# Second half of layer 0: LayerNorm's powers for four tiles at once, gathers ahead of stores, and rows kept for eight tiles

## The reference

```python
edge_index = jnp.stack([src, dst])
h = jnp.maximum(_layernorm(x, axis=-1), 0.0)
x = x + _L0_gnn_ref(h, edge_index, L0_gnn_W1, L0_gnn_b1, L0_gnn_W2, L0_gnn_b2)
...
def gnn_layer(x, W, b, src, dst):
    h = x @ W.T + b
    msgs = h[src]
    agg = jax.ops.segment_sum(msgs, dst, num_segments=N_NODES)
    return jax.nn.relu(agg)
h = gnn_layer(x, W1, b1, src, dst)
out = gnn_layer(h, W2, b2, src, dst)
```

## Time and profile before

| | |
|---|---|
| median of 3 runs | 2921.37 us (2920.29 to 2921.51) |
| the profiled execution | 2921.05 us, span 2919.0 us |
| granted TensorE clock, mean | 0.982 |
| busy: TensorE, VectorE, ScalarE, GpSimd | 89%, 70%, 46%, 60% of the span |
| second half of layer 0, first to last `add_x` | 769.0 to 1136.0 us |

### The profile page before, as it was taken

How to read it: one execution, slowest core, us unless ns; L and a number is a source line. 1 busy time by engine, 2 the same in 40 slices (tenths; PEclk the granted TensorE clock), 3 DMA queues, 4 the chain that set the end, 5 groups by cost and what they waited for, 6 DMA issues and landing times. The chain is left out here.

```text
span 2919.0 us, 51172 instructions
## 1 busy us (share of the span) xinstructions
PE 2596.8 (89%) x13954; PEld 2165.5 (74%) x13954; DVE 2056.6 (70%) x5472; ACT 1354.5 (46%) x2798; POOL 1754.9 (60%) x1917
## 2 busy tenths in 40 slices
PE   3677729999799996999999979999999889999998
PEld 2344427888677775889999967888888768888886
DVE  7688846666466564677778877888888746666666
ACT  0555414444455554655555534333333245555554
POOL 0455525555477776677777747877777555555554
PEclk9999999999899998999999999999999989999999
DMA  9544453333344444333333314443333255555553
GB/s 291 195 147 161 147 167 92 104 115 121 107 130 141 152 154 154 102 113 116 109 117 116 118 61 137 125 122 112 110 116 115 73 143 153 153 152 154 151 154 114
DMA packets 146573, 387.71 MB, mean 133 GB/s; under 512 B 34423, under 2 KB 35383, under 8 KB 145882
## 3 DMA queue, kind: packets, MB, share of 16 engines
q0 software_dynamic: 101408, 304.38, 35.0%
q1 hardware_dynamic: 44010, 80.12, 8.3%
q10 hardware_dynamic: 1056, 2.10, 0.2%
HBM read 261.74 MB, written 149.28 MB: 141 GB/s over the span
## 5 line engine op out<-in xcount | busy, mean ns | idle before, releaser
L1517 PE MATMUL c_pu<-c_Zhi,parts 128*128 128x256 f32 x640 | 182.3, 285 | 10.2 <-DVE c_Zlo L1442 10.2
L1519 PE MATMUL c_pu<-c_Zhi,parts 128*128 128x256 f32 x640 | 181.6, 284 | 0.0
L787 POOL DMA_INDIRECT f_Gsrc<-rows,indexS x80 | 80.6, 1007 | 166.3 <-PE f_phsrc L2013 160.4
L1518 PE MATMUL c_pu<-c_Zlo,parts 128*128 128x256 f32 x640 | 180.5, 282 | 0.0
L1955 DVE TENSOR_TENSOR f_Hlosrc<-f_phsrc,f_Hhisrc 128x512 fp32r<-128x512 f32 x80 | 55.4, 692 | 167.9 <-ACT f_Hhisrc L1925 137.2
L1931 ACT ACTIVATE f_Mhi<-f_pm 128x512 fp32r<-128x512 f32 x80 | 47.9, 599 | 267.2 <-DVE f_pm L1964 253.8
L791 POOL DMA_INDIRECT h<-a_rows,indexD x80 | 80.5, 1007 | 125.2 <-ACT a_rows L1103 116.9
L1679 ACT CAST d_Hhi<-d_ph 128x512 fp32r<-128x512 f32 x80 | 46.8, 585 | 227.7 <-PE d_ph L1793 222.9
L767 PE MATMUL a_po<-parts,a_Thi 128*128 128x512 f32 x320 | 132.6, 414 | 5.5 <-DVE a_Tlo L1135 5.4
L1409 ACT ACTIVATE c_pu<-c_pu,c_b1col 128x256 f32<-128x256 f32 x160 | 61.8, 450 | 162.9 <-PE c_pu L1519 162.9
L426 POOL DMA_INDIRECT edgesD<-r_cargoD,r_posiD x80 | 76.9, 961 | 97.0 <-ACT r_cargoS L473 40.4
(11 more groups left out here) (434 smaller groups left out, 9801.9 us busy)
## 6 DMA issues: line engine op xcount, KB each, us to landing
rows<-r_xt SPq DMA_DIRECT2D x20, 1040.0 KB
h<-q_zerorow SPq DMA_DIRECT2D x80, 256.0 KB, 2.3
r_xt<-in_x SPq DMA_DIRECT2D x80, 256.0 KB
selrowsD<-selD SPq DMA_DIRECT2D x1, 2640.0 KB
selrowsS<-selS SPq DMA_DIRECT2D x1, 2640.0 KB
q_keyrowD<-in_dst POOLq DMA_DIRECT2D x1, 2560.0 KB
q_keyrowS<-in_src POOLq DMA_DIRECT2D x1, 2560.0 KB
o_wstage<-in_L_W ACTq DMA_DIRECT2D x2, 1024.0 KB
```

The costliest lines, as they stand in the source:

```text
L787: return pool.indirect_dma_start(out, None, table, bass.IndirectOffsetOnAxis(ap=rows, axis=0))
L1517: pe.matmul(psum_u[:, o, :], g.Whi[2][:, c, cols], Zhi[:, c, :], start=c == 0, stop=False)
L1518: pe.matmul(psum_u[:, o, :], g.Whi[2][:, c, cols], Zlo[:, c, :], start=False, stop=False)
L1519: ins = pe.matmul(psum_u[:, o, :], g.Wlo[2][:, c, cols], Zhi[:, c, :], start=False, stop=c == C - 1)
```

## The change

In the second half of layer 0 the class `Norm` now takes a group of four tiles in place of two: VectorE's two small operations and GpSimd's power and multiply cover 128x4. `b_rows` has eight slots instead of four, and with it GpSimd's and VectorE's code is unrolled over eight tiles. A tile's order on GpSimd was store of T-2, G of T+4, xr of T+2, with power and multiply for T-2 and T-1 ahead of each pair. It is now G of T+4, xr of T+2, store of T-4, with power and multiply for T-4 to T-1 ahead of each four. The constant zeros behind the rows are written by one fill in place of four. `layer1` and `layer2` keep groups of two, and the first half of layer 0 keeps its order.

```diff
 class Norm:
-    def __init__(self, e, name, moved):
-        self.moved = moved
+    def __init__(self, e, name, moved, group=2):
+        self.moved, self.group, self.places = moved, group, 2 * group
...
     def finish(self, dve, tick, T):
-        s = T.slot(4)
-        wait(dve, self.s_bias if self.moved else self.s_scale, T.use(2) - 1)
+        s = T.slot(self.places)
+        some = slice(s - self.group + 1, s + 1)
+        wait(dve, self.s_bias if self.moved else self.s_scale, T.use(self.group) - 1)
...
-        if T.j % 2:
+        if T.j % self.group == self.group - 1:
             dve.wait_ge(self.s_mean, T.t + 1)
-            dve.tensor_scalar(self.var[:, s - 1:s + 1], self.mean_var[:, s - 1:s + 1, 1], LN_EPS, None, ALU.add)\
+            dve.tensor_scalar(self.var[:, some], self.mean_var[:, some, 1], LN_EPS, None, ALU.add)\
...
     def make_scales(self, pool, T, neg_half, scales):
-        s = T.slot(4)
-        pool.wait_ge(self.s_var, T.t // 2 + 1)
-        pool.tensor_tensor(scales, self.var[:, s:s + 2], neg_half[:, :], ALU.pow).then_inc(self.s_scale, 1)
+        s = T.slot(self.places)
+        pool.wait_ge(self.s_var, T.t // self.group + 1)
+        pool.tensor_tensor(scales, self.var[:, s:s + self.group], neg_half[:, :], ALU.pow).then_inc(self.s_scale, 1)
...
+    QUAD, RING = 4, 8 if second else 4
...
-        rows = e.sb("rows", [P, U, EXT if second else D], F32)
+        rows = e.sb("rows", [P, RING, EXT if second else D], F32)
...
             def body(i):
-                for pair in (0, 2):
-                    if second:
-                        at(i, pair, -2, U, NT, scales)
-                    for u in (pair, pair + 1):
+                if second:
+                    for u in range(RING):
+                        if u % QUAD == 0:
+                            at(i, u, -QUAD, RING, NT, scales)
+                        at(i, u, 4, RING, NT, start_fetch)
+                        at(i, u, 2, RING, NT, residual)
+                        at(i, u, -QUAD, RING, NT, store)
+                else:
+                    for u in range(U):
                         at(i, u, -2, U, NT, store)
                         at(i, u, 4, U, NT, start_fetch)
-                        if second:
-                            at(i, u, 2, U, NT, residual)
...
             def add_x(T):
-                s, r = T.slot(2), T.slot(U)
+                s, x, r = T.slot(2), T.slot(U), T.slot(RING)
                 dve.wait_ge(s_prod, T.t + 1)
-                dve.wait_ge(s_x[T.slot(U)], 16 * (T.use(U) + 1))
-
-                wait(dve, s_put[r], 16 * T.use(U))
+                dve.wait_ge(s_x[x], 16 * (T.use(U) + 1))
+
+                wait(dve, s_put[r], 16 * T.use(RING))
...
-            pipeline(dve, GR, 1, 1, body)
+            pipeline(dve, NT // RING, 1, 1, body)
```

More of the change, by code:

```diff
@@ L795 @@
 class Norm:
-    def __init__(self, e, name, moved):
-        self.moved = moved
+    def __init__(self, e, name, moved, group=2):
+        self.moved, self.group, self.places = moved, group, 2 * group
         self.stats = e.ring(name + "stats", 2, [P, 6], F32)
-        self.mean_var = e.sb(name + "mv", [P, 4, 2], F32)
-        self.var = e.sb(name + "var", [P, 4], F32)
-        self.minus = e.sb(name + "minus", [P, 4], F32) if moved else None
+        self.mean_var = e.sb(name + "mv", [P, self.places, 2], F32)
+        self.var = e.sb(name + "var", [P, self.places], F32)
+        self.minus = e.sb(name + "minus", [P, self.places], F32) if moved else None
         self.s_stats, self.s_mean, self.s_var, self.s_minus, self.s_scale, self.s_bias = (
@@ L807, in mean @@
     def mean(self, T):
-        return self.mean_var[:, T.slot(4), 0:1]
+        return self.mean_var[:, T.slot(self.places), 0:1]
     def statistics(self, dve, T, rows):
@@ L932, in layer0 @@
             brow = e.sb("brow", [P, D], F32)
[L933 removed]
+        neg_half = e.sb("neghalf", [P, QUAD], F32)
         G = e.ring("G", U, [P, D if second else EXT], F32)
@@ L937, in layer0 @@
         Thi, Tlo = e.ring("Thi", 2, [P, C, P], F32R), e.ring("Tlo", 2, [P, C, P], F32R)
-        rows = e.sb("rows", [P, U, EXT if second else D], F32)
+        rows = e.sb("rows", [P, RING, EXT if second else D], F32)
         xr = e.ring("xr", U, [P, D], F32) if second else None
-        ln = Norm(e, "ln", True) if second else None
+        ln = Norm(e, "ln", True, QUAD) if second else None
         W = None if second else Weights(nc, e, g, [(2, io.L1_W1), (3, io.L1_W2)])
@@ L1008, in scales @@
             def scales(T):
-                s = T.slot(U)
-                ln.make_scales(pool, T, neg_half, rows[:, s:s + 2, SCALE])
-                ln.make_biases(pool, T, rows[:, s:s + 2, SCALE], rows[:, s:s + 2, BIAS])
+                some = slice(T.slot(RING), T.slot(RING) + QUAD)
+                ln.make_scales(pool, T, neg_half, rows[:, some, SCALE])
+                ln.make_biases(pool, T, rows[:, some, SCALE], rows[:, some, BIAS])
             def store(T):
-                s = T.slot(U)
+                s = T.slot(RING)
                 if second:
-                    pool.wait_ge(ln.s_bias, T.t // 2 + 1)
+                    pool.wait_ge(ln.s_bias, T.t // QUAD + 1)
                 else:
@@ L1040, in _ @@
             if second:
-                for s in range(U):
-                    pool.memset(rows[:, s, BIAS + 1:EXT], 0.0).then_inc(s_const, 1)
-            pool.wait_ge(s_const, 3 + U if second else 3)
-            straight(GR, 1, 1, body, between=W and (lambda n: W.split_low(pool, n)))
-            for s in range(U):
-                pool.wait_ge(s_put[s], 16 * GR)
+                pool.memset(rows[:, :, BIAS + 1:EXT], 0.0).then_inc(s_const, 1)
+            pool.wait_ge(s_const, 4 if second else 3)
+            straight(NT // RING, 1, 1, body, between=W and (lambda n: W.split_low(pool, n)))
+            for s in range(RING):
+                pool.wait_ge(s_put[s], 16 * (NT // RING))
         @block.scalar
@@ L1155, in norm_rows @@
                 dve.wait_ge(s_rows, T.t + 1)
-                ln.statistics(dve, T, rows[:, T.slot(U), 0:D])
+                ln.statistics(dve, T, rows[:, T.slot(RING), 0:D])
             def finish_rows(T):
```

38 lines of the change are left out of this document (19 added, 19 removed).

## The result

The changed kernel takes 3032.97 us (median of 4 runs, 3029.61 to 3033.53) against 2920.83 us of the kernel before in the same comparison (4 runs, 2918.23 to 2921.51): ratio 1.0381, 95% interval 1.0366 to 1.0396. It is 112 us **slower**, where 33 us less were forecast. The profiled execution has a span of 3031.6 us, 112.6 more than before.

A forecast was written before the change was run, and what follows sets the result against it. GpSimd was taken to bound layer 0's second half at 4.67 us a tile, TensorE able to do 4.15. The stretch falls from 367.0 to 327.9 + 2.8, -36.3, plus 3.0 at the end: -33.3, so 2888 us, range 2884 to 2896.

The forecast's parts named there:

- What bounds the kernel: Layer 0's second half: GpSimd, never paused by other engines, sets 9.33 us a pair; VectorE waits 3.17 us for late G.
- GpSimd's terms: GpSimd's work per four tiles falls from 18.66 to 16.75 us, with power 1.12 and gap behind the multiply 0.18.
- B: Rival: the 0.86 us gap behind GpSimd's multiply stays; 17.43 us a four, 19.7 saved, 2901 us; chance 0.08.
- What TensorE gets: At TensorE's 4.15 us a tile the stretch takes 327.9 us, 39.1 less, with 2.8 left over for GpSimd falling behind.
- C: Rival: gathers behind one power come too late; loop 15.7 us, 17.7 with landings 2 us later; 2906 us; chance 0.07.
- E: Rival: slower, C's loop exceeding 18.66 us, needing landings more than 3.0 us later than 3.57; 2944 us; chance 0.04.
- The end of the stage: Four stores instead of two follow the last power before the next stage's barrier: 3.0 us later.
- VectorE's loop body and the eight places: VectorE's doubled loop body and row slots reused after eight tiles were forecast to cost nothing.

The follow-up runs named there:

- e4: Kernel before, groups of two kept, only the order inside a tile changed to G, xr, store: 2974.87 us, ratio 1.0185.
- e9: Kernel before without the powers and their small multiply in this stage; a store waits for its rows alone: 2950.91 us, ratio 1.0102.
- e10: e4 with an idle power over two columns added behind the multiply of the biases, lengthening the pause: 58 us faster than e4.
- e8: Kernel after with groups of two and, per tile, the store of four tiles ago first, then G, xr: time between those of e6 and e10.
- e12: Kernel before with a third, unread gather per tile on GpSimd in layer 0's first half: 3004.59 us, ratio 1.0271.
- e3: Kernel before with only eight places for rows and VectorE's code written out for eight tiles: 2918.09 us, ratio 0.9993.
- e7: Kernel after with gathers of G and xr fetching four columns a row in place of 512: 3036.31 us in one run.
- e5: e4 with an idle multiply over two columns added behind the multiply of the biases, lengthening the pause: 2980 us.
- e6: e4 with an idle multiply over 120 columns added behind the multiply of the biases, lengthening the pause: 2969 us.

## Why the prediction was wrong

**What bounds the kernel: the step that failed.** "VectorE meanwhile stands still for 3.17 us until a DMA has landed ... So the late thing is G, and it is late because GpSimd is." The wait was for TensorE's count, held back by GpSimd's issuing; the profile's releaser was a guess, and the sum's own record, ended 2.7 us before VectorE resumed, spoke against it. From this followed the wrong conclusion that time saved on GpSimd comes back one for one. GpSimd did set 9.33 us a pair, but its 0.86 us in front of the store, and the power itself, were also the pause in which TensorE's counts got through (e4 and e9: with less of it the kernel is slower, e10: with it back, as fast).

**GpSimd's terms held.** The power 1.05 us for 1.12, the gap 0.15 for 0.18, the four's work 16.69 for 16.75. B was rightly given little, though its reason was only part of it: in e8 a store that doesn't wait for the multiply still stands 0.59 us behind it, so most of the 0.86 us belongs to the store and not to the wait.

**What TensorE gets, 4.15 us a tile, failed.** The pace holds where GpSimd pauses by itself: in the stage's first tiles and in layer 0's first half, the two places from which I took it (e12 takes it away there too). Neither could show what twelve issues in a row do.

**The loop of C was the right place with the wrong size.** I priced power to variance at 15.7 us, with a landing of 3.57 in it, and said that E needed landings more than 3 us later. It is 24.79: 16.69 from the power to the end of the last issue, 2.09 until VectorE sees the held count, 5.75 for VectorE's two tiles up to the variance (851.64 to 857.39; C had 2.8 for one tile), 0.26 to the power. No landing is in it; the term that I left out is that the loop runs behind the whole run of issues, with the held count at its end. The 18 fours of the steady part carry the loss of 110 us. E, given 0.04, happened by its sign and its condition (the loop longer than 18.66), through another cause.

**TensorE's clock** fell with the waits, from 1.00 to 0.85 of full in the mean (behind such a stop, from 852 to 856 us, the granted clock is 0.50, the lower of its two levels, and a matmul over 512 columns takes 0.63 us; at 1.00, from 857 us on, it takes 0.39). I take it for a consequence: the path through VectorE's two tiles takes 5.75 us after and 5.64 before (879.77 to 885.41).

**The end of the stage** was forecast at +3.0 and measured +2.5. **VectorE's loop body and the eight places** cost nothing, as forecast (e3).

The Trainium skill (Perfetto Trace Analysis, Tensor Engine Instruction) says that the end of a matmul in the profile is estimated, and that the semaphore goes out only when PSUM has acknowledged all writes; that acknowledgement stands in no record. This case's rows agree that a count can come long behind the record's end, up to 10.5 us; which step is held back they do not tell. The Trainium skill (Perfetto Trace Analysis, DMA Instruction — SWDGE (GPSIMD)) says that what the profile shows of an issue on GpSimd is its cores writing descriptors and not data moving. e7 agrees with it: a small part of the bytes, the same issue times, the same holding.

**Left open:** what in the chip holds TensorE's counts while GpSimd issues, and why some of them come through in the middle of a run. Whether counts are held as long without the profiler isn't shown either: every run here has its span and its granted clock from a profile. Whether the number of rows per transfer matters was not tried, nor was a version that spends the pause on something useful. No kernel here beats the one before by more than 0.2%.

## What to carry to other kernels

Before removing idle or slow work from GpSimd, check what happens in that pause: compare the end of TensorE's matmul with the start of the instruction that waits for it, and both with GpSimd's runs of indirect transfers. Where they lag until a run ends, as here, GpSimd's pauses are part of the critical path, and long unbroken runs of issues are dear; six issues and 1.9 us of something else was here better than twelve and one longer pause, and better than six with 0.5 us less (e5, 1.35 us). A releaser named "remote", or a DMA that the waiting instruction has no use for, is a question and not an answer.

## What the runs showed of the hardware

- TensorE's semaphore counts reached VectorE up to 10.5 us after the matmul's recorded end while GpSimd issued indirect transfers 0.3 us apart. Those that waited for its stop came 1.25 to 1.45 us after the end of the last of six issues (the kernel before), 1.8 to 2.3 us after the last of twelve (after); others came through in the middle of a run, 0.4 to 5.1 us late (after). VectorE's and ScalarE's counts came within 0.03 us in the same run.
- Of pauses between runs of six issues, those of 1.21 and 1.35 us let no waiting count through (24 of 24, e4 and e5), those of 1.54 us all (11 of 11, e6).
- The holding did not change when the gathers moved 16 bytes a row in place of 2048.
- A power on GpSimd takes 0.74 us for 128x2, 1.05 for 128x4 and 1.37 for 128x6: about 0.16 us for each further column, on 0.42.
- The issue of a gather on GpSimd follows arithmetic 0.15 to 0.18 us later. That of a store follows 0.81 to 0.86 us later where it waits for that arithmetic, and 0.59 us later where it doesn't (e8).
